# Mixture of experts on one NeuronCore: token rows scattered to their slots in DRAM before the expert blocks, the blocks load them with plain DMAs, and every unit of the shared expert runs before the blocks

## What is computed

```
router_logits = x @ gate_w.T
probs = jax.nn.softmax(router_logits, axis=-1)
topk_w, topk_idx = jax.lax.top_k(probs, K)                  # K = 6
topk_w = topk_w / jnp.sum(topk_w, axis=-1, keepdims=True)
combine = jnp.sum(jax.nn.one_hot(topk_idx, E, dtype=x.dtype) * topk_w[..., None], axis=1)
h = jax.nn.silu(jnp.einsum('th,eih->tei', x, experts_w1))
y = jnp.einsum('tei,ehi->teh', h, experts_w2)
routed_out = jnp.einsum('teh,te->th', y, combine)
g, u = jnp.split(x @ shared_gate_up.T, 2, axis=-1)
shared_out = jax.nn.silu(g) * u @ shared_down.T
return (routed_out + shared_out).reshape(orig_shape)
```

## Time and profile before

| | us |
|---|---|
| median of 3 runs | 2336.49 (2335.48 to 2339.5) |
| the profiled execution: its own time | 2341.23 |
| its span | 2339.4 |
| the mixture's front, first work to the first transposed row | about 1309 to 1371 |
| its 111 blocks | about 1371 to 1712 |
| its end | 1712 to about 1740 |

### The profile page before, as it was taken

How to read it: one execution, slowest core, us unless ns; L and a number is a source line. 1 busy time by engine, 2 the same in 40 slices (tenths; PEclk the granted TensorE clock), 3 DMA queues, 4 the chain that set the end, 5 groups by cost and what they waited for, 6 DMA issues and landing times. The chain is left out here.

```text
span 2339.4 us, 44802 instructions
## 1 busy us (share of the span) xinstructions
PE 2069.6 (88%) x13047; PEld 1769.7 (76%) x13047; DVE 1555.0 (66%) x4486; ACT 1248.2 (53%) x3126; POOL 801.0 (34%) x1400
## 2 busy tenths in 40 slices
PE   5698879799999995899999878788769999987998
PEld 3454467578999992699999767777658999986887
DVE  6699857766788884788888742111147888885665
ACT  4699933656766662566666312222216666653332
POOL 4433310203333320333433176665613333311221
PEclk9789989899999997799999888898979999997999
DMA  1157020102211204000000147776740000004331
GB/s 64 37 111 205 1 90 1 68 3 93 75 65 59 74 19 147 5 2 0 0 0 1 45 137 207 204 204 189 208 165 22 21 20 16 18 9 120 110 110 52
DMA packets 132903, 174.08 MB, mean 74 GB/s; under 512 B 43868, under 2 KB 99140, under 8 KB 130088
## 3 DMA queue, kind: packets, MB, share of 16 engines
q1 hardware_dynamic: 121704, 140.27, 20.7%
q0 software_dynamic: 10656, 29.11, 3.9%
q10 hardware_dynamic: 416, 3.15, 0.3%
HBM read 155.57 MB, written 36.83 MB: 82 GB/s over the span
## 5 line engine op out<-in xcount | busy, mean ns | idle before, releaser
L2548 DVE COPY l2f_x_t<-bank 128x256 f32<-128x256 f32 x111 | 47.1, 424 | 273.5 <-PE bank L2278 145.2
L1292 ACT ACTIVATE l0a_prob<-bank,l0a_shift 128x496 f32<-128x496 f32 (+1 forms) x256 | 161.0, 1158 | 2.4 <-DVE l0a_shift L1316 2.3
L723 ACT ACTIVATE l1a_prob<-l1a_masked,l1a_shift,l1a_q_scale 128x512 f32<-128x512 f32 x128 | 104.5, 816 | 75.3 <-DVE l1a_shift L781 73.2
L2423 POOL DMA_INDIRECT l2f_x_rows_of<-l2f_x_rows,l2f_table x111 | 108.1, 974 | 90.0 <-remote 34.4
L2290 PE MATMUL bank<-l2f_x_t,l2f_w 128*128 128x128 f32 x888 | 129.0, 293 | 9.6 <-issue 9.5
L2379 ACT ACTIVATE l2f_h<-bank 128x128 f32<-128x128 f32 x111 | 30.8, 277 | 198.1 <-PE bank L2290 101.9
L723 ACT ACTIVATE l2a_prob<-l2a_masked,l2a_shift 128x512 f32<-128x512 f32 x128 | 92.7, 724 | 78.5 <-DVE l2a_shift L785 75.7
L723 ACT ACTIVATE l3a_prob<-l3a_masked,l3a_shift 128x512 f32<-128x512 f32 x128 | 92.8, 725 | 78.1 <-DVE l3a_shift L785 75.2
L2290 PEld LDWEIGHTS bank<-l2f_x_t,l2f_w 128*128 128x128 f32 x888 | 118.7, 208 | 12.6 <-issue 12.5
L2428 POOL DMA_INDIRECT l2f_y_rows<-l2f_y,l2f_target x111 | 110.6, 996 | 41.2 <-issue 33.7
L1292 ACT ACTIVATION_READ_ACCUMULATOR l0a_prob<-bank,l0a_shift 128x1 f32 x256 | 124.3, 889 | 0.0
(11 more groups left out here) (590 smaller groups left out, 7753.2 us busy)
## 6 DMA issues: line engine op xcount, KB each, us to landing
l2f_w<-w_rows SPq DMA_DIRECT2D x111, 304.0 KB
l1a_side<-rms SPq DMA_DIRECT2D x16, 1024.0 KB, 4.8
w_rows<-in_l2f_w SPq DMA_DIRECT2D x4, 2048.0 KB
l2f_hots<-l2f_y_rows SPq DMA_DIRECT2D x8, 768.0 KB, 11.2
l3f_raw<-in_l3f_w SPq DMA_DIRECT2D x24, 256.0 KB, 3.9
l3f_mix<-shares SPq DMA_DIRECT2D x16, 384.0 KB, 3.6
l2f_w_rest<-in_l2f_w SPq DMA_DIRECT2D x111, 48.0 KB
w_rows<-in_l2f_w SPq DMA_DIRECT2D x8, 512.0 KB
```

Source lines behind the costliest of these rows:

```text
L723: act.activation(prob[:, unit, :], masked[:, unit, :], ACT.Exp, bias=shift[:, unit:unit + 1], scale=q_scale[:, slot, t:t + 1] if qk_norm e ...
L1292: last = act.activation(prob[:, at, q, first:end], score_bank[at % 2 * 2 + q][:, first:end], ACT.Exp, bias=shift[:, at, q, part:part + 1], ...
L2423: pool.indirect_dma_start(x_rows_of[:, b % of.X_SLOTS, :], None, x_rows, bass.IndirectOffsetOnAxis(table[:, b:b + 1], 0)).then_inc(gathere ...
L2548: dve.tensor_copy(x_t[:, b % 2, :], turn_bank[b % 2][:, 0:D]).then_inc(x_kept, 1)
```

## The change

A new DRAM tensor `x_slots` has one row for each of the 111 x 128 slots. During the attention of the third layer SP fills it with copies of the input x, so that slots that nobody uses hold finite numbers. In the mixture GpSimd issues 48 indirect DMAs (eight token tiles by six choices), each of which scatters 128 rows of `x_n` to their slots. The blocks' rows are then contiguous, and ScalarE loads them with a plain DMA for each block: six before the loop, and the one for block b+6 after the SiLU of block b. `table`, the store of `x_rows` and the gathers are gone. VectorE makes all 48 `in_block`, since GpSimd now scatters at that time. All twelve units of the shared expert run before the blocks, the last two pairs of tiles with their product on VectorE, and the shared result is added to x straight from PSUM. The scatter of the results follows each block at once, and the diagonals begin at block 24.

The core of the diff:

```diff
@@ heads_stage, SP, stage l2a
                     if made:
+                        m.issue_fill(sp)
                         return
+def fill_slots(nc, m, x):
+    rows = Grouped.BLOCKS * P
+    m.x_slots = nc.dram_tensor("x_slots", (rows, D), F32, kind="Internal").ap()
+    firsts = range(0, rows, TOKENS)
+    def issue(sp):
+        for first in firsts:
+            count = min(TOKENS, rows - first)
+            sp.dma_start(m.x_slots[first:first + count, :], x[0:count, :]).then_inc(m.slots_filled, 16)
@@ SP
-                sp.wait_ge(norm.xn_done, TT)
-                sp.dma_start(x_rows.rearrange("(t p) d -> p t d", p=P), m.x_n[:]).then_inc(x_stored, 16)
@@ TensorE
                 def turn(b):
-                    pe.wait_ge(gathered[b % of.X_SLOTS], 16 * (b // of.X_SLOTS + 1))
+                    pe.wait_ge(x_loaded[b % of.X_SLOTS], 16 * (b // of.X_SLOTS + 1))
...
-                shared_out(0)
-                shared_out(1)
                 for t in range(TT):
-                    pe.wait_ge(pool_hots, (t + 1) * of.POOL_HOTS)
                     for k in range(chosen):
...
-                last.then_inc(table_ready, 1)
-                pe.wait_ge(pair_kept, of.EARLY * of.SHARED)
-                pe.wait_ge(shared_y_kept, of.EARLY * 2)
+                last.then_inc(targets_ready, 1)
+                shared_out(0)
+                shared_out(1)
+                for pair in range(of.EARLY, pairs):
+                    shared_in(pair)
+                for pair in range(of.EARLY, pairs):
+                    shared_out(pair)
+                pe.wait_ge(pair_kept, shared_units)
+                pe.wait_ge(added, TT)
...
-                    if b in of.LATE_IN:
-                        late_in(of.LATE_IN.index(b))
-                    if b in of.LATE_OUT:
-                        late_out(of.LATE_OUT.index(b))
@@ ScalarE
+                for pair in range(pairs):
+                    shared_in(pair)
+                def load_rows(b):
+                    wait_for(act, x_turned, b - of.X_SLOTS + 1)
+                    act.dma_start(x_rows_of[:, b % of.X_SLOTS, :], x_slots[b * P:(b + 1) * P, :]).then_inc(x_loaded[b % of.X_SLOTS], 16)
+                act.wait_ge(x_placed, 16 * TT * chosen)
+                for b in range(of.X_SLOTS):
+                    load_rows(b)
                 for b in range(blocks + 1):
...
+                        if b + of.X_SLOTS < blocks:
+                            load_rows(b + of.X_SLOTS)
@@ GpSimd
+                pool.wait_ge(m.slots_filled, m.fill_count)
                 pool.wait_ge(part_done, 1)
                 for t in range(TT):
-                    for k in range(of.POOL_HOTS):
-                        pool.tensor_scalar(in_block[:, t * chosen + k, :], row[:], part[:, 0, t * 8 + k:t * 8 + k + 1], None,
-                                           ALU.is_equal).then_inc(pool_hots, 1)
-                pool.wait_ge(x_stored, 16)
-                pool.wait_ge(table_kept, 1)
+                    for k in range(chosen):
+                        pool.indirect_dma_start(x_slots, bass.IndirectOffsetOnAxis(slot_i[:, t, k:k + 1], 0), m.x_n[:, t, :],
+                                                None).then_inc(x_placed, 16)
+                pool.wait_ge(targets_kept, 1)
...
-                for b in range(blocks + of.Y_LAG):
-                    if b < blocks:
-                        gather(b)
-                    if b >= of.Y_LAG:
-                        scatter(b - of.Y_LAG)
+                for b in range(blocks):
+                    scatter(b)
@@ VectorE
-                    if k >= of.POOL_HOTS:
-                        dve.tensor_scalar(in_block[:, n, :], row[:], part[:, 0, of_slot:of_slot + 1], None, ALU.is_equal)
+                    dve.tensor_scalar(in_block[:, n, :], row[:], part[:, 0, of_slot:of_slot + 1], None, ALU.is_equal)
...
+                def add_shared(pair):
+                    for n in range(2):
+                        t = 2 * pair + n
+                        dve.wait_ge(shared_y_ready, t + 1)
+                        dve.tensor_tensor(m.x[:, t, :], m.x[:, t, :], y_bank[n][:, 0:D], ALU.add).then_inc(added, 1)
+                for pair in range(of.EARLY):
+                    add_shared(pair)
+                for pair in range(of.EARLY, pairs):
+                    shared_multiply(pair)
+                for pair in range(of.EARLY, pairs):
+                    add_shared(pair)
```

More of the change, by code:

```diff
@@ L2053 @@
     W_SLOTS, X_SLOTS, Y_SLOTS = 6, 6, 6
-    Y_LAG = X_SLOTS + 3
     SPREAD = 8
-    POOL_HOTS = 4
     EARLY = 2
-    LATE_IN = tuple(range(10, 58, 8))
-    LATE_OUT = tuple(range(62, 78, 4))
     BY_PRODUCT = 3
+    DIAGONALS_AT = 24
 def repack_grouped(nc, m, dram):
@@ L2093, in repack_grouped @@
     return issue
+def fill_slots(nc, m, x):
+    rows = Grouped.BLOCKS * P
+    m.x_slots = nc.dram_tensor("x_slots", (rows, D), F32, kind="Internal").ap()
+    m.slots_filled = nc.alloc_semaphore(name="slots_filled")
+    firsts = range(0, rows, TOKENS)
+    m.fill_count = 16 * len(firsts)
+    def issue(sp):
+        for first in firsts:
+            count = min(TOKENS, rows - first)
+            sp.dma_start(m.x_slots[first:first + count, :], x[0:count, :]).then_inc(m.slots_filled, 16)
+    return issue
 def grouped_mixture(nc, m, dram, name):
@@ L2098, in grouped_mixture @@
     experts, chosen, blocks, rest_of = of.EXPERTS, of.CHOSEN, of.BLOCKS, of.REST
-    x_rows = nc.dram_tensor(name + "_x_rows", (TOKENS, D), F32, kind="Internal").ap()
+    x_slots = m.x_slots
     y_rows = nc.dram_tensor(name + "_y_rows", (TOKENS * of.SPREAD + blocks * P, D), F32, kind="Internal").ap()
@@ L2144, in grouped_mixture @@
         target = st.sbuf("target", [P, blocks], I32)
-        source_i = st.sbuf("source_i", [P, blocks], I32)
-        table = st.sbuf("table", [P, blocks], I32)
         equal = st.sbuf("equal", [P, 2, TT, experts])
@@ L2177, in grouped_mixture @@
         w_loaded = [st.sem(f"w_loaded{n}") for n in range(of.W_SLOTS)]
-        gathered = [st.sem(f"gathered{n}") for n in range(of.X_SLOTS)]
+        x_loaded = [st.sem(f"x_loaded{n}") for n in range(of.X_SLOTS)]
         y_stored = [st.sem(f"y_stored{n}") for n in range(of.Y_SLOTS)]
         part_done, padded = st.sems("part_done", "padded")
-        late_ready, late_gate_done, late_h_done, late_out_ready = st.sems("late_ready", "late_gate_done", "late_h_done", "late_out_ready")
         diagonals_done, part_ready, part_added = st.sems("diagonals_done", "part_ready", "part_added")
@@ L2198, in _, with load_weights @@
                 sp.dma_start(shared_w[:], dram["shared_w"].rearrange("u p n -> p u n")).then_inc(shared_loaded, 16)
-                sp.wait_ge(norm.xn_done, TT)
-                sp.dma_start(x_rows.rearrange("(t p) d -> p t d", p=P), m.x_n[:]).then_inc(x_stored, 16)
                 sp.wait_ge(m.repacked, m.repack_count)
                 sp.wait_ge(owner_kept, 1)
-                for b in range(blocks):
+                def load_weights(b):
                     slot = b % of.W_SLOTS
@@ L2244, in shared_out @@
                         t = 2 * pair + n
-                        wait_for(pe, shared_y_kept, t - 1)
+                        wait_for(pe, added, t - 1)
                         for u in range(of.SHARED):
@@ L2249, in shared_out @@
                         last.then_inc(shared_y_ready, 1)
-                def late_in(s):
-                    pair, u = of.EARLY + s // of.SHARED, s % of.SHARED
-                    if s == 0:
-                        pe.wait_ge(owner_kept, 1)
-                    wait_for(pe, late_h_done, s)
-                    for up in range(2):
-                        first = (2 * D + P) * up
-                        for c in range(DC):
-                            last = pe.matmul(logit_bank[:, up * 2 * P:(up + 1) * 2 * P], shared_w[:, u, first + c * P:first + (c + 1) * P],
-                                             m.x_t[:, c, pair * 2 * P:(pair + 1) * 2 * P], start=(c == 0), stop=(c == DC - 1))
-                    last.then_inc(late_ready, 1)
-                def late_out(n):
-                    pair = of.EARLY + n // 2
-                    if n == 0:
-                        pe.wait_ge(table_kept, 1)
-                    pe.wait_ge(late_h_done, (n // 2 + 1) * of.SHARED)
-                    wait_for(pe, added, 2 * of.EARLY + n)
-                    for u in range(of.SHARED):
-                        last = pe.matmul(place_bank[:, 0:D], shared_h[:, pair % 2, u, n % 2 * P:(n % 2 + 1) * P],
-                                         shared_w[:, u, D:2 * D], start=(u == 0), stop=(u == of.SHARED - 1))
-                    last.then_inc(late_out_ready, 1)
                 def turn(b):
-                    pe.wait_ge(gathered[b % of.X_SLOTS], 16 * (b // of.X_SLOTS + 1))
+                    pe.wait_ge(x_loaded[b % of.X_SLOTS], 16 * (b // of.X_SLOTS + 1))
                     wait_for(pe, x_kept, b - 1)
@@ L2359, in shared_in @@
```

(6 more changed lines are left out.)

51 lines of the change are left out of this document (15 added, 36 removed).

## The result

| | kernel before | changed kernel |
|---|---|---|
| median, beside each other on one chip | 2335.98 us (2330.53 to 2339.5) | 2271.55 us (2269.22 to 2274.74) |
| ratio, 95% interval | | 0.9727 (0.9703 to 0.9751) |
| span of the profiled execution | 2339.4 us | 2267.4 us |
| the whole stage of the mixture | 428.6 us | 357.0 us |
| its start to the first turned row | 61.6 us | 111.4 us |

The change makes the kernel 64 us faster. The forecast had the direction, with 38 us, but the lower end of its range, 2277, lay 5.5 us too high. All other stages together differ by 0.4 us, the attention with the fill included, so the fill costs nothing that shows. The 72 us of the spans are +49.8 in front, -120.0 in the blocks and -1.4 at the end.

What follows compares the result with a forecast made beforehand. The prediction took semaphores of TensorE held beside GpSimd's gathers to bound the blocks. From 2339.4 us, +38 in front and -76 in the blocks gave 2301.4, or 2298 on the median's scale; own range 2276 to 2315, eight in ten 2277 to 2376.

Steps and rivals of the forecast that it cites:

- the fill: Attention before the mixture: SP's 14 copies of 1 MB, 45 us of transfers, cost nothing; 45 us as bound above.
- the DMA term of the blocks: Blocks: 2.15 us of DMA work a block, at a share of 0.92, makes 2.35 us a block.
- Where the holds come from: Blocks: TensorE's semaphores reach ScalarE and VectorE late, likeliest because of GpSimd's gathers; scatters do no harm in the tail.
- What the holds cost: Blocks: TensorE loses 44.1 us directly and more at a lower clock; all sums start from the profiled span, 2339.4 us.
- GpSimd follows the pace and doesn't set it: Blocks: GpSimd needs 2.57 us a block, but its gathers wait for others, so it isn't the bound.
- The blocks, -76 us: From the first SiLU 111 blocks at 2.35 us plus 4 us: 265 us instead of 341.
- The front, +38 us: Before the blocks: 48 scatters take 61.9 us, so the first transposed row comes at about 1409 instead of 1371.0.
- The second rival: Front: VectorE's one-hots stop GpSimd's scatters, up to 30 us more, 2328 us; chance of over 10 us 0.12.
- The first rival: Blocks: all DMA traffic together sets the pace, so it stays 3.00 to 3.07 us, 2370 to 2374 us; chance 0.30.
- the end: End of the stage: same instructions, the last scatter waits for the last y in both kernels, so no change.
- ScalarE's room for the row loads: Blocks: ScalarE is busy 0.77 us a block; a load's 0.33 us more leaves it idle almost half of 2 us.

Runs made afterwards that it cites:

- four_ways: Changed kernel with its blocks in four ways: one scatter; scattered twice; gathered and stored plainly; gathered and scattered. 2339.5 us, kernel before 2332.5 beside it.
- light_after: Changed kernel whose wide weight load brings 256 of 608 columns a row from the seventh block on: 2262.6 us, kernel before 2278.0 beside it.
- after_again: Changed kernel, unchanged, run again on another chip, without waits on remote in the mixture: 2262.3 us, ratio 0.9925 to the kernel before.

## Why the prediction was wrong

Two steps failed. What puts the time below the range is the DMA term of the blocks, 2.15 us of work divided by 0.92; what was wrong in the mechanism is where the holds come from.

**Where the holds come from: wrong.** The step that failed is "I take the gathers, which come from GpSimd's queue and write into SBUF beside the weight loads, as the likeliest cause; the scatters ... do no harm there". four_ways shows gathers alone, one a block, without a hold, and scatters alone, two a block, with them. The tail of the earlier trace rows misled me: after the last gather most scatters no longer stood 0.3 us behind another indirect DMA (from 1696.7 to 1702.9 us 1.3 to 2.9 us behind), which four_ways makes the likelier reason than their direction. The earlier trace rows misled me too: a hold need not end with GpSimd's queue, since two of the front's end in an unbroken row of scatters. The direction of the loop's forecast was right by luck in the cause: the change takes out one of two, and either would have done.

**What the holds cost: not to be seen in one profile.** Every sum started from 2339 us as if it were the program's time. On five chips the same program took 2277 to 2281 us (the one trace of it there has no holds), in the forecast's runs and three later sets 2331 to 2336. Two of those sets, at different times, were on one chip, which speaks for the chip and against the moment. Of the 64 us, 16 to 18 us are there without holds as well (2280.1 or 2278.7 to 2262.3), and the rest, some 48 us, is what the old order loses to the holds and the new one doesn't: about 57 us before, 9 us after. What makes a chip one or the other isn't shown.

**GpSimd follows the pace and doesn't set it: right for that profile only.** Its own 2.57 us a block stood in the earlier trace rows, and it is the bound as soon as the holds are gone (2.57 measured). So a kernel before without holds would have had 281 us of blocks, and the 38 us of front would have eaten most of the gain. The forecast never asked for the second bound behind the first.

**The blocks, -76 us: mis-sized by 44.** Measured -120.0. The term that failed is 2.15 us of DMA a block, divided by 0.92 to 2.35. The share of the earlier trace rows counts how long packets are under way, and it isn't a fixed amount of work: the same bytes are 0.98 x 1.98 = 1.94 us a block in the changed kernel from 1480 to 1600, and light_after, with 176 KB less a block, has the same pace. The 0.92 was a guess that no row showed. TensorE's 1.98 us of the earlier trace rows was the floor, and it stood in the forecast. 111 x (2.35 - 1.98) = 41 us of the 44.

**The front, +38 us: mis-sized by 12 on that chip.** 111.4 for 61.6 us, +49.8. On an undisturbed chip it is 103.7 for 61.0 us, +42.7, so that 4.7 us are the terms and the other 7 the holds beside the scatters. The terms, in after_again: the first scatter starts at 1342.3, the last leaves at 1407.9, 65.6 us for the 61.9 of the sum. Issue, landing and first load are as forecast (1409.40, 1411.50 for 1406.6, 1409). The shared units, given until about 1400, are done at 1384.7 there, well under the cover of the scatters; with the holds the cover is gone (their sums end at 1419.6).

**The second rival, scatters slowed by VectorE: small.** 48 scatters take 50.3 us where the median is 0.963 us each: 50.3 - 46.2 = 4.1 us, with a maximum of 1.469 us. All but one of the slow ones lie before 1363.6 us, where VectorE ends its one-hots. The 30 us for a GpSimd that stands still don't come. By the Trainium skill's rule (SBUF — State Buffer, the box on the "DVE blocks DMA" trap) the time would be near 2328; the trace agrees with its direction, with 4 us for it.

**The first rival, the sum of the DMA traffic: wrong,** and with its 0.30 it pulled the range to 2376, where the lower end had no room. A block at TensorE's own 1.98 us (224 us for the blocks, 2257 on the median's scale) was in no case, though the earlier trace rows showed it, and only the longer front brought the time near the range. **The fill, the end, ScalarE's room for the row loads:** right. A load costs 0.33 us of issue, and ScalarE delays nobody: TensorE's idle time in the blocks is 1.5 us.

## What to carry to other kernels

Where a profile shows idle time with no releaser in the program, take the time of the same program on other chips before pricing a change by it, and ask what is the bound if that time is gone. A share of busy DMA engines is no amount of work that stays when the pace changes: look for an engine that waits for a transfer, and without one take the next engine's own time as the floor. On some chips TensorE's semaphores can be held beside indirect DMAs that stand 0.3 us apart on GpSimd; with 0.84 us between each two of them, or one in 1.98 us, no kernel here waits on remote.

## What was not expected of the hardware

One program takes 2277 to 2281 us on five chips and 2331 to 2336 us on at least two others. Between the two traces of it 60.0 of 61.9 us lie in the blocks, where one has waits on remote and the other none.

Beside an unbroken row of scatters the semaphores of TensorE came 9 to 25 us after the matmuls that raise them. In the changed kernel's front ScalarE wakes at 1383.26, 1397.99 and 1412.70, 14.73 and 14.71 us apart, with scatters going on at an even 1.27 us before and after the first two. TensorE's own lines there, each set of eight matmuls raising the semaphore that ScalarE waits for (the first line holds three sets):

```profile
1369.16 5.34 PE L2248 MATMUL bank<-l2g_x_t,l2f_shared_w 128*128 128x256 f32 x24
1376.21 1.99 PE L2248 MATMUL bank<-l2g_x_t,l2f_shared_w 128*128 128x256 f32 x8 [1.71 <-issue]
1383.96 3.55 PE L2248 MATMUL bank<-l2g_x_t,l2f_shared_w 128*128 128x256 f32 x8 [5.75 <-issue]
```

The three waits are for the third, fourth and fifth set, which end at 1374.5, 1378.2 and 1387.5 in the profile: 8.8, 19.8 and 25.2 us before ScalarE wakes. TensorE starts a set only when ScalarE has copied the set before last (1383.96 behind the copy of 1383.54), so one late semaphore delays the next work too. In four_ways one such wait was 39.5 us. VectorE starts 0.4 us behind the start of ScalarE's copy in the same stretch (1383.94 after 1383.54), so ScalarE's semaphores are in time. What raises the held ones in the end stays open.
